# Softmax denominators of two attention layers: sent through memory and inverted packed by ScalarE, instead of gathered and spread by TensorE and inverted by VectorE

## The reference, cut to what matters

```
scores = q @ k^T * scale          (1024 queries x 1024 keys)
p      = exp(scores - max over the keys)
out    = (p @ v) / (sum of p over the keys)
```

## Time and profile before

| | |
|---|---|
| median of 3 runs | 2347.7 us (2345.77 to 2347.72) |
| the profiled execution | 2346.99 us, span 2345.1 us |
| TensorE busy | 2157.1 us, 92% of the span |
| VectorE, ScalarE, GpSimd busy | 1634.2, 1362.7 and 184.4 us (70%, 58%, 8%) |
| a0's softmax stage, from its first product with bank turns to the last copy-out | about 46.5 to 700.4 us |
| a1's | about 809 to 1153.8 us |

### The profile page before, as it was taken

How to read it: one execution, slowest core, us unless ns; L and a number is a source line. 1 busy time by engine, 2 the same in 40 slices (tenths; PEclk the granted TensorE clock), 3 DMA queues, 4 the chain that set the end, 5 groups by cost and what they waited for, 6 DMA issues and landing times. The chain is left out here.

```text
span 2345.1 us, 42550 instructions
## 1 busy us (share of the span) xinstructions
PE 2157.1 (92%) x16840; PEld 991.6 (42%) x16840; DVE 1634.2 (70%) x2062; ACT 1362.7 (58%) x2668; POOL 184.4 (8%) x371
## 2 busy tenths in 40 slices
PE   5899999999999689999989999999999989999999
PEld 3232333233334222222336666666666534444454
DVE  6999999999954599999465555555555365555553
ACT  3689888888883368888744444445444332222243
POOL 3000000000001500000000000000000010000000
PEclk7899999999999889999999999999999999999998
DMA  4000000001000200010000000000000014545520
GB/s 142 13 13 6 13 15 12 6 14 31 2 1 0 82 28 22 10 47 2 2 4 1 5 5 5 1 5 20 1 1 1 1 41 110 124 115 122 127 61 18
DMA packets 48515, 72.07 MB, mean 31 GB/s; under 512 B 10629, under 2 KB 35077, under 8 KB 44368
## 3 DMA queue, kind: packets, MB, share of 16 engines
q1 hardware_dynamic: 46324, 67.98, 11.3%
q10 hardware_dynamic: 668, 1.04, 0.1%
q0 software_dynamic: 1344, 0.52, 0.1%
HBM read 61.70 MB, written 7.88 MB: 30 GB/s over the span
## 5 line engine op out<-in xcount | busy, mean ns | idle before, releaser
L908 ACT ACTIVATE a0p<-ps 128x512 f32<-128x512 f32 x1024 | 541.9, 599 | 112.2 <-PE ps L812 97.7
L918 DVE TENSOR_REDUCE a0nm<-ps 128x2 f32<-128x1024 f32 x512 | 587.5, 1213 | 11.3 <-PE ps L792 9.1
L826 PE MATMUL ps<-a0p,a0vst 128*32 128x256 f32 x4096 | 327.8, 392 | 25.9 <-ACT a0p L908 14.2
L908 ACT ACTIVATE a1p<-ps 128x512 f32<-128x512 f32 x512 | 274.8, 596 | 68.5 <-PE ps L812 60.0
L918 DVE TENSOR_REDUCE a1nm<-ps 128x2 f32<-128x1024 f32 x256 | 295.0, 1215 | 11.2 <-PE ps L792 10.4
L812 PE MATMUL ps<-a0qm,a0k 32*128 32x512 bf16 x1024 | 273.7, 387 | 0.1
L1672 DVE TENSOR_REDUCE canm<-ps 128x1 f32<-128x128 f32 (+7 forms) x256 | 182.1, 753 | 115.1 <-PE ps L1509 114.5
L792 PE MATMUL ps<-a0k,a0q 32*128 32x512 bf16 x1024 | 203.5, 396 | 27.9 <-DVE a0nm L918 21.8
L1908 ACT ACTIVATE ex_s<-ps 128x512 f32<-128x512 f32 x128 | 76.4, 597 | 253.0 <-PE ps L1863 253.0
L1616 ACT ACTIVATE cap_long<-ps,canm 128x1024 f32<-128x1024 f32 (+3 forms) x128 | 121.4, 952 | 174.7 <-DVE canm L1672 174.7
L792 PE MATMUL ps<-a1k,a1q 64*128 64x512 bf16 x512 | 150.1, 404 | 26.5 <-DMA a1k<-a1mask 14.4
(11 more groups left out here) (302 smaller groups left out, 2681.9 us busy)
## 6 DMA issues: line engine op xcount, KB each, us to landing
ex_wb<-ex_w_dram SPq DMA_DIRECT2D x62, 512.0 KB, 6.3
a0parts<-a0parts_sb SPq DMA_DIRECT2D x8, 384.0 KB, 3.5
a1parts<-a1parts_sb SPq DMA_DIRECT2D x8, 384.0 KB, 3.5
f2wg<-in_ex_gate SPq DMA_DIRECT2D x32, 64.0 KB, 1.8
f2wu<-in_ex_up SPq DMA_DIRECT2D x32, 64.0 KB, 1.9
f2wd<-in_ex_down SPq DMA_DIRECT2D x32, 64.0 KB, 1.9
mod_w<-in_L_wmod SPq DMA_DIRECT2D x4, 384.0 KB, 6.5
a0q<-a0parts SPq DMA_DIRECT2D x62, 24.0 KB
```

Of the source, the lines that this page charges most:

```text
L826: last = pe.matmul(R.ps[32 * j:32 * j + 32, 6, cols], vst[:, g, s, j * HG // 4, :], p[:, s % 2, j, cols], start=(g == 0 and s == 0 and hal ...
L908: act.activation(p[:, s % 2, e, :], R.ps[:, score_bank(n), :], ACT.Exp).then_inc(exp_done, 1)
L918: dve.tensor_reduce(nm[:, u % 2, tb, 2 - 2 * z:4 - 2 * z, hf], R.ps[:, bank:bank + 2, :], X_AXIS, ALU.max, negate=True).then_inc(bank_free, 1)
```

## The change

The turns `den` and `spread` of all pairs but the last chunk are gone, and `turns` holds only maxima, transposes and one last `spread`. In their place each chunk `n` (two to a pair) makes a round through memory. SP waits for ScalarE's copy-out (`pv_out`), stores the 8 denominator rows of `o` to memory (`den_dram`), waits for that to land, and loads them back as 128 rows of 32 (`packed`). ScalarE inverts them there with an Ln (`log`, in step 5 of the unit after its first Exp) and an Exp with scale -1 (`invert`, in step 5 after its third Exp). SP stores the inverses, waits, and loads them back with each row repeated 16 times into `rec`, which now is the norm's tile `R.xc`. GpSimd multiplies (`divide`, behind the `split` of that unit). SP's loads of the next groups' queries and keys now stand behind the fourth transfer of the odd chunk. The last chunk of a stage is spread as it is by one fp32 product of 512 columns, inverted by ScalarE's Ln and Exp on 128 x 512, and multiplied by VectorE.

```diff
-    rec = sb("rec", [128, 128])
+    rec = R.xc
+    packed = sb("packed", [128, 2, 32])
...
-        for kk in range(2, PAIRS):
-            sp.wait_ge(exp_done, (kk - 1) * 128)
-            for g in range(2):
-                load_group(A, 2 * kk + g, (kk % 2) * 2 + g, sp)
+        for n in range(2 * PAIRS - 1):
+            kk, c, times = n // 2 + 2, n % 2, 16 * (n // 2 + 1)
+            sp.wait_ge(pv_out, n + 1)
+            sp.dma_start(den_dram[c], o[8::16, c, :]).then_inc(den_out[c], 16)
+            sp.wait_ge(den_out[c], times)
+            sp.dma_start(packed[:, c, :], den_dram[c].rearrange("r (a t) -> (r a) t", a=16)).then_inc(den_packed[c], 16)
+            sp.wait_ge(inverted, n + 1)
+            sp.dma_start(rec_dram[c].rearrange("r (a t) -> (r a) t", a=16), packed[:, c, :]).then_inc(rec_out[c], 16)
+            sp.wait_ge(rec_out[c], times)
+            sp.dma_start(rec[:, c, :], rec_dram[c].unsqueeze(1).broadcast_to([8, 16, CW])).then_inc(rec_in[c], 16)
+            if c and kk < PAIRS:
+                sp.wait_ge(exp_done, (kk - 1) * 128)
+                for g in range(2):
+                    load_group(A, 2 * kk + g, (kk % 2) * 2 + g, sp)
...
+        def divide(n):
+            pool.wait_ge(rec_in[n % 2], 16 * (n // 2 + 1))
+            t0 = n % 2 * CW
+            pool.tensor_tensor(A.on[:, n // 2, t0:t0 + CW], o[:, n % 2, :], rec[:, n % 2, :], ALU.mult).then_inc(divided, 1)
...
             split(u + 1)
+            if u and u % 2 == 0:
+                divide(u // 2 - 1)
...
-        def den(kk):
...
-        def spread(n):
...
+        def spread():
+
+            pe.wait_ge(pv_out, 2 * PAIRS)
+            pe.matmul(R.ps[:, wait_bank("spread"), :], den_spread[:], o[:, 1, :], start=True, stop=True).then_inc(bank_full, 2)
...
             if kk:
-                act.wait_ge(bank_free, emptied("spread", 2 * (kk - 1) + c))
+                act.wait_ge(divided, 2 * (kk - 1) + c + 1)
             act.activation(o[:, c, :], R.ps[:, 6, :], ACT.Copy).then_inc(pv_out, 1)
+
+        def log(n):
+
+            act.wait_ge(den_packed[n % 2], 16 * (n // 2 + 1))
+            act.activation(packed[:, n % 2, :], packed[:, n % 2, :], ACT.Ln).then_inc(logged, 1)
+
+        def invert(n):
+
+            act.wait_ge(logged, n + 1)
+            act.activation(packed[:, n % 2, :], packed[:, n % 2, :], ACT.Exp, scale=-1.0).then_inc(inverted, 1)
...
+                    if u and u % 2 == 0 and s == 5 and e == 0:
+                        log(u // 2 - 1)
+                    if u and u % 2 == 0 and s == 5 and e == 2:
+                        invert(u // 2 - 1)
         take(PAIRS - 1, 1)
+        act.wait_ge(bank_full, filled("spread"))
+        act.wait_ge(divided, 2 * PAIRS - 2)
+        act.activation(rec[:, 1, :], R.ps[:, dve_bank("spread"), :], ACT.Ln).then_inc(last_rec, 1)
+        act.wait_ge(last_rec, 1)
+        act.activation(rec[:, 1, :], rec[:, 1, :], ACT.Exp, scale=-1.0).then_inc(last_rec, 1)
...
-        invert(PAIRS - 1)
-        divide(2 * PAIRS - 2)
-        divide(2 * PAIRS - 1)
+        divide_last()
```

More of the change, by code:

```diff
@@ L659, in softmax_stage @@
     v_ready, pool_step = sem("v_ready"), sem("pool_step")
+    den_out, den_packed, rec_out, rec_in = [[sem("%s%d" % (w, i)) for i in range(2)]
+                                            for w in ("den_out", "den_packed", "rec_out", "rec_in")]
+    logged, inverted, divided, last_rec = (sem(n) for n in ("logged", "inverted", "divided", "last_rec"))
+    den_dram, rec_dram = (nc.dram_tensor(pre + n, [2, 8, CW], F32, kind="Internal").ap() for n in ("den", "rec"))
     def place(u):
@@ L676, in ahead, with turns_at @@
         return [x if x[0] < UNITS else None for x in slots]
[L678 to L687, removed]
+    def turns_at(u, s):
+        return s == 6 and u + 1 < UNITS
     turns = [("max", 0, i) for i in range(16)] + [("max", 1, i) for i in range(4)] + [("turn", 0)]
@@ L865, in on_pe @@
             for s in range(8):
-                slots, extra = ahead(u, s), special(u, s)
+                slots = ahead(u, s)
                 before = (u, s - 1) if s else (u - 1, 7)
@@ L879, in on_pe @@
                     pv(*before, 1)
[L880 to L885, removed]
+                if turns_at(u, s):
+                    turn(u + 1)
         for half in range(2):
             pv(UNITS - 1, 7, half)
-        den(PAIRS - 1)
-        spread(2 * PAIRS - 2)
-        spread(2 * PAIRS - 1)
+        spread()
     def on_act(act):
@@ L964, in on_dve @@
                     reduce(*slots[1])
-                if extra and extra[0] == "turn":
-                    merge(extra[1])
-                if extra and extra[0] == "den":
-                    invert(extra[1])
-                if extra and extra[0] == "spread":
-                    divide(extra[1])
-        invert(PAIRS - 1)
-        divide(2 * PAIRS - 2)
-        divide(2 * PAIRS - 1)
+                if turns_at(u, s):
+                    merge(u + 1)
+        divide_last()
     return Programs(sp=on_sp, pool=on_pool, pe=on_pe, act=on_act, dve=on_dve)
@@ L2225, in softmax_weights @@
             W.loads += [(W.bqk[:, i:i + 1], dram[f"L1_b{n}"]) for i, n in enumerate("qk")]
[L2226 to L2230 removed]
+        W.den_spread = shared.den_spread if shared else W.add("den_spread", [128, 128], dram["den_spread"])
         if layer == 0:
```

47 lines of the change are left out of this document (11 added, 36 removed).

## The result

The changed kernel takes 2309.56 us (median of 4 runs, 2306.39 to 2315.48) against 2346.73 for the kernel before on the same chip (2345.2 to 2347.72): a ratio of 0.9845, 95% interval 0.9824 to 0.9866, 37 us less. The forecast was 2319.4 in 2308 to 2337. The profiled execution took 2309.85 us, its span 2307.9.

What follows compares the result with a forecast made beforehand. VectorE was taken to set the pace of the softmax stages. Removing 38.8 us less 11.2 us of added waits gave 27.6 us gained against 2346.99: 2319.4 us, range 2308 to 2337.

Steps and rivals of the forecast that it cites:

- The removed work: Softmax stages: old division's excess goes, 3.32 us a pair in a0 and 3.63 in a1, with ends 38.8 us.
- The ends: Stage ends, last copy-out to next stage's first product: 3.83 us instead of 6.11 and 6.21, together 4.7 us gained.
- VectorE sets the pace: Softmax units: VectorE busy 18.60 of a0's 18.79 us, TensorE's products following its beat; a1's TensorE nearly full too.
- The place of the added waits: Late denominators only in even chunks behind a set of loads: six times in a0, twice in a1.
- The loads: SP's moved loads begin 16.3 us later in their pair than now, hidden by some 18 us.
- Their size: Added waits in both stages sum to 11.2 us, from late denominators and small activations.
- The transfers: Each round's memory transfers: 2.4 us a store, 1.9 a load; denominators late by 1.1 us in a0, 2.8 in a1.
- The activations: ScalarE's two small activations a round, 0.43 us, cost 0.1 a round in a0 and 0.3 in a1.
- What a wait passes on: TensorE held 1.5 and 3.2 us; about 1 absorbed in a0, 0.6 in a1, leaving 0.6 and 2.6 each.
- GpSimd against VectorE: Rival: GpSimd's products hold up VectorE, 22 x 1.20 = 26.4 us, 2346 us, no change; chance 0.05.
- The rule that I weighed: GpSimd and VectorE share a locked SBUF port pair, but reductions never take it; lock alone would lose 22 products of 1.2 us.

Runs made afterwards that it cites:

- their experiment: Both engines' old division work put back into the changed kernel as three more turns of the shared bank pairs per pair of groups: 2339.9 us, ratio 0.9969.
- the two versions without waits: Changed kernel with SP's set of loads cut in two (2305.92 us), and changed kernel with the even chunks' Ln and Exp at step 6 (2305.79 us).

## Why the prediction was right, and what it mis-sized

**The removed work: right.** 3.32 a pair in a0 and 3.63 in a1 are what the pairs lost, exactly but for the late units: 23.1 and 10.9 us against 23.2 and 10.9. Taking the excess of whole units, and not a sum of instructions, paid: VectorE's rows (0.96 + 2 x 0.69) give 2.34 of the 3.32, and 0.9 of the rest is the turns of the banks, as their experiment shows. The ends gave 4.5 of the 4.7.

**"VectorE sets the pace": too simple.** In a0 TensorE's small products alone cost a pair 2.27 us, more than VectorE's alone (1.90), and with both back it is 2.33; in a1 they cost 3.42 of 3.63. The busy times hint at it: with TensorE's work back, a1's second unit has TensorE busy in 19.91 of 19.93 us. The chain goes through both engines, and their costs overlap rather than add. The sum didn't depend on it, but a forecast for a change that removes VectorE's part alone would have.

**The place of the added waits: right.** Only even chunks behind a set of loads are late, SP held 29.9 us (30.0), the Ln due after 10.07 (10.2). The loads begin 15.2 us later in their pair than before (16.3), at no cost: 13.6 behind the copy-out instead of 1.6 ahead of it.

**Their size: the term that was off.** 11.2 us forecast, 5.05 measured, in three parts. (1) The transfers. I took 2.4 us for a store and 1.9 for a load from larger ones. The term that was off is the store of the inverses, ahead of the loads: 1.42. With its follower's issue it brings the loads 1.1 us forward. The two transfers behind the loads took 2.54 and 1.6 and give only some 0.3. So the denominators come in 9.9 us behind the copy-out instead of 11.3, and five of a0's six rounds are just in time instead of 1.1 late. The sixth is late because its store of the inverses took 3.59 us (below). In a1 the lateness was 1.71 and 2.19, not 2.8. The Trainium skill's "DMA: Bandwidth & Descriptors", "Anatomy of one DMA", puts the fixed part of a transfer at about 2.0 us, fitted to transfers that GpSimd issues; here SP issues them, and the landing's median was 1.7 for the load and 1.4 for the store, so the measurement decides, below the page. (2) The activations: forecast 0.1 and 0.3 a round, 2.4 in all. Units with them and no wait last 19.03 and 19.68 to 19.69, as units with a copy-out did before: nothing, but for 0.16 and 0.23 in the last units. (3) What a wait passes on. I let TensorE absorb 1 us in a0 and 0.6 in a1. At a clock of 1.00 it absorbs 0.44 in a0 with the Ln in step 4 (1.74 to 1.30, 1.13 to 0.69) and 0.58 with it in step 5 (in the repeated kernel 1.14 to 0.56, with the doubled product 1.02 to 0.44), and 0.15 in a1 (1.71 to 1.56, 2.19 to 2.04). This error went the other way: with rounds as late as forecast, the lateness would have cost more than I gave it.

**GpSimd against VectorE: fell, as forecast.** 22 products of 1.27 us lie beside reductions with 1208/1214/1226 ns as minimum, median and maximum in a0, median and maximum the same as in the earlier trace rows; doubled, they cost nothing. The rule that I weighed, the Trainium skill's "SBUF — State Buffer", "Who interferes with whom", lets a reduction pass beside GpSimd, and now 22 large products bear it out.

**The distance from forecast to result**, 37.2 us of span against 27.6: 6.2 more by the added waits, 0.3 less by the removed work, and 3.7 more by parts without changed work. The last 3.7 is luck as far as can be told: parts that vary by 3 to 6 us from profile to profile with the same code, the start and the end with the granted clock. Without it the forecast would have been off by 5.9 us and the time some 2313.

**The one late round of a0.** It is the same in the profiles of the changed kernel, of its repetition and of the doubled product, and longest with the earlier Ln. In the profile after it stands behind the second of the sets that follow a round (SP's queue again):

```profile
241.16 0.33 SPq L733 DMA_DIRECT2D a0rec<-a0packed  x1
244.75 0.63 SPq L735 DMA_DIRECT2D xc_res<-a0rec  x1
```

The store of the inverses took 3.59 us to the next issue instead of 1.42 (165.50 to 166.92), and the loads behind it began 2.2 later. The DMA view from 241.1 to 244.8 us shows what else ran:

```profile
q8 instruction: 1, 0.02, 1.5%
a0rec<-a0packed SPq DMA_DIRECT2D x1, 16.0 KB, 3.6
```

A 16 KB transfer of instructions lies beside the store, from 242.68 to 243.56 by the trace's packets. Of the store's 144 packets 135 are done before it; the last nine start at 243.54, as it ends. The same holds in all six profiles in which this store took 2.97 to 3.59 us: each has one such transfer beside it, and the last nine packets start within 0.02 us of its end. With VectorE's old work back the same store has none beside it and took 1.42. Where TensorE's old work is back, the transfer meets the store one set earlier (2.61 to 3.06 us), and there the Ln behind that set is the late one, by 0.37 to 0.72 us. Nine is a sixteenth of 144, one of the 16 DMA engines' share, so the store's part on one engine seems to have waited for the code on it; the records don't name the engine. No run moves the code to try it, and why the transfer falls there is open.

**Open.** Why the stretch ahead of a1's first merge varies by 6.5 us under the same code was not tried.

## What to carry to other kernels

Price a removed step by whole units with it less whole units without it; that number held to 1%, where instructions alone made 70% of it. Small transfers that stand in one queue with a long set of loads are late by the set's rest, and the cure is to cut the set around them or to ask for the result a little later: either removed all late units here, 5 us of them (2305.9 and 2305.8 us). What stands ahead of the set counts as much: there a transfer of 1.4 us for 2.4 brought five rounds in on time, and one of 3.6 made the sixth late. Before moving work from one engine's list, ask whether the other engine's share of the same step holds up the unit by itself.

## What the runs showed of the hardware

A wait can cost more than its length, because TensorE's granted clock falls behind it. With the earlier Ln, TensorE had no product to do for 3.38 us (first the timeline of TensorE, then stretches of 2 us of the same unit):

```profile
279.61 0.60 PE L829 MATMUL ps<-a0qm,a0k 32*128 32x512 bf16 x1 [3.38 <-ACT a0p L915]
...
280.70 1.08 PE L843 MATMUL ps<-a0p,a0vst 128*32 128x256 f32 x8
```

```profile
276.00:278.00 2.00, 0.23 (x6) 0.00 (x0) 1.38 (x2) 0.00 (x0) 0.00 (x0) 1.00 0.05 17
278.00:280.00 2.00, 0.39 (x3) 0.20 (x3) 0.00 (x0) 1.16 (x4) 0.00 (x0) 0.80 0.05 7
280.00:282.00 2.00, 2.00 (x16) 0.41 (x13) 1.32 (x2) 1.62 (x5) 0.24 (x1) 0.50 0.05 8
```

The same group of eight at the full clock, in TensorE's timeline of the profile after:

```profile
278.18 0.64 PE L843 MATMUL ps<-a0p,a0vst 128*32 128x256 f32 x8
```

The clock stands at 0.50, the 1.2 GHz level, from the first products behind the idle time on, and eight value products take 1.08 us instead of 0.64. Something like it happened in the late unit of a0 in the profile after: TensorE was without a product for 1.05 us up to 279.87, and from 281.59 on its products take 0.60 instead of 0.39 (0.94 over the unit). The wait of 1.41 cost 1.45, where 1.41 - 0.58 = 0.83 would have been due. In a1 the waits of 1.71 and 2.19 left the clock at 1.00. In the repeated kernel a1's first wait did too (1.96, cost 1.82), but the second, 1.90, cost 2.79 at 0.94. So one and the same lateness has no steady price from one execution to the next. That goes with the spread of the runs, 9 us for the changed kernel (2306.39 to 2315.48) and some 2 for the two versions without waits; that the one comes from the other is argued, not shown.

A small store can wait for the program's own code. In the nine stores named above (2.61 to 3.59 us to the next issue instead of 1.42), the last nine of 144 packets start only when a 16 KB transfer of instructions, 0.88 to 1.43 us long, ends.
